# Order of scores, reciprocals and rotary sums within each part of the layer 2 self-attention of a four-layer decoder on one Trainium2 core

## The reference, cut to what matters

```
qkv = jnp.einsum('bsd,dhf->bshf', x, w_qkv) + b_qkv
q, k, v = jnp.split(qkv, 3, axis=-1)
q = q * cos + _rotate_half(q) * sin
k = k * cos + _rotate_half(k) * sin
...
scores = jnp.einsum('bhqd,bhkd->bhqk', q, k) / jnp.sqrt(jnp.float32(f))
...
scores = scores + alibi[None]
scores = jnp.where(causal == 0, -1000000000.0, scores)
weights = jax.nn.softmax(scores, axis=-1)
attn = jnp.einsum('bhqk,bhkd->bhqd', weights, v).transpose(0, 2, 1, 3)
return jnp.einsum('bshd,hdm->bsm', attn, w_out) + b_out
```

## Time and profile before

| what | value |
|---|---|
| median of 3 runs | 3147.62 us (3141.78 to 3148.28) |
| the profiled execution, its own time | 3148.16 us |
| its span in the profile | 3146.4 us |
| mean granted TensorE clock | 0.861 of full |
| stretch of this self-attention | some 1508 to 2030 us of the span |
| PE, DVE, ACT, POOL busy in that stretch | 424.41, 244.59, 312.20, 275.52 us of 522.00 |

### The profile page before, as it was taken

The page is one execution under the profiler, slowest core; times in us unless marked ns, Lnnn a source line. Parts: engine busy times, 40 slices in busy tenths (PEclk is TensorE's granted clock), DMA queues, the critical chain, the costliest instruction groups (busy, mean ns, idle before and its releaser), DMA issues. The chain is left out here.

```text
span 3146.4 us, 40958 instructions
## 1 busy us (share of the span) xinstructions
PE 2411.6 (77%) x12416; PEld 1417.6 (45%) x12416; DVE 1811.8 (58%) x4431; ACT 1239.4 (39%) x2575; POOL 534.3 (17%) x509
## 2 busy tenths in 40 slices
PE   6763976666768998699688888775888879578587
PEld 4653642224623323366344444453444456557454
DVE  4666347778855576444544444345666643745777
ACT  2442342224344454322466666523444422223212
POOL 0410000003310000000455555342000000043100
PEclk7875977777879999799799999877999989688799
DMA  0000000001010000000322222000000000100000
GB/s 32 31 6 0 1 5 0 0 0 44 1 55 1 0 0 0 0 0 0 97 69 68 68 68 68 22 31 24 1 0 0 0 1 0 56 23 1 1 1 14
DMA packets 19876, 61.81 MB, mean 20 GB/s; under 512 B 4928, under 2 KB 4928, under 8 KB 18592
## 3 DMA queue, kind: packets, MB, share of 16 engines
q1 hardware_dynamic: 19488, 59.53, 6.0%
q10 hardware_dynamic: 256, 0.68, 0.1%
HBM read 42.37 MB, written 1.05 MB: 14 GB/s over the span
## 5 line engine op out<-in xcount | busy, mean ns | idle before, releaser
L689 DVE TENSOR_REDUCE MF<-P 128x1 f32<-128x512 f32 (+3 forms) x512 | 282.3, 587 | 97.4 <-PE P L479 53.3
L824 ACT ACTIVATE PT<-P 128x512 f32<-128x512 f32 (+3 forms) x512 | 244.2, 516 | 232.5 <-PE P L496 123.0
L2318 PE MATMUL P<-XT,W 128*128 x424 | 221.0, 618 | 63.4 <-ACTq L2352 63.4
L2394 DVE SCALAR_TENSOR_TENSOR X<-P,WE,X 128x128 f32 x576 | 162.5, 344 | 167.0 <-PE P L2335 162.0
L2335 PEld LDWEIGHTS P<-W,e_h 128*128 128x128 f32 (+1 forms) x1952 | 220.7, 191 | 61.1 <-issue 53.2
L2335 PE MATMUL P<-W,e_h 128*128 128x128 f32 (+1 forms) x1952 | 227.8, 278 | 3.3 <-DVE X L2394 3.3
L1286 POOL TENSOR_TENSOR d_e<-d_e,d_rc 128x512 f32<-128x512 f32 (+3 forms) x256 | 178.2, 723 | 223.1 <-DVE d_rc L1193 223.0
L2363 ACT ACTIVATE e_g<-P 128x512 f32<-128x512 f32 x148 | 88.4, 597 | 310.5 <-PE P L2318 310.5
L496 PE MATMUL P<-QA,KA 128*128 128x512 bf16 (+3 forms) x512 | 180.2, 358 | 32.6 <-ACT PT L824 12.7
L479 PE MATMUL P<-KA,QA 128*128 128x512 bf16 (+3 forms) x512 | 182.2, 362 | 28.3 <-ACT KA L808 15.1
L541 PE MATMUL P<-PT,VA 128*32 128x512 f32 (+3 forms) x1024 | 195.8, 518 | 0.0
(11 more groups left out here) (359 smaller groups left out, 4635.5 us busy)
## 6 DMA issues: line engine op xcount, KB each, us to landing
d_bt<-in_alibi SPq DMA_DIRECT2D x32, 512.0 KB, 3.7
d_moved<-d_raw SPq DMA_DIRECT2D x256, 64.0 KB, 2.0
W<-in_w_L_xattn SPq DMA_DIRECT2D x1, 4291.0 KB, 14.1
W<-in_w_L_ffn SPq DMA_DIRECT2D x1, 3333.0 KB, 11.1
W<-in_w_L_ffn SPq DMA_DIRECT2D x1, 3155.0 KB, 10.2
W<-in_w_L_attn SPq DMA_DIRECT2D x1, 2636.0 KB, 11.6
W<-in_w_L_ffn SPq DMA_DIRECT2D x1, 2310.0 KB, 9.0
W<-in_w_L_ffn SPq DMA_DIRECT2D x1, 1744.0 KB, 6.9
```

The costliest lines, as they stand in the source:

```text
L689: last = v.tensor_reduce(col, src, AX.X, ALU.max, negate=True)
L824: a.activation(k.PT[0:self.kp, h % self.slots, t, N - w:N], src, ACT.Exp, scale=self.scale).then_inc(s("exp_done"), 1)
L2318: pe.matmul(P[:, PG + j % 2, :], w["w1"][:, col:col + 128], x, start=True, stop=True).then_inc(s("gate"), 1)
L2394: last = v.scalar_tensor_tensor(x, y, k.WE[:, bass.ds(c * 4 + t, 1), e], x, ALU.mult, ALU.add)
```

## The change

On PE, `scores` moves from before `values`, `result` and `weighted` to the end of each part. On DVE, both calls of `recip` move ahead of `biased`. On POOL, `rope` moves ahead of `shares`. ACT and SP stay as they are. No instruction is added or taken away, and every wait stays with its instruction.

```diff
@@ PE, line 1145
                     if 0 <= n - 3 < ITEMS:
                         turn(n - 3, j)
-                    if 0 <= n - 2 < ITEMS:
-                        scores(n - 2, j)
                     if j == 1 and 0 <= n - 2 < ITEMS:
                         values(n - 2)
                     if j == 1 and 0 <= n - 5 < ITEMS:
                         result(n - 5)
                     if 0 <= n - 4 < ITEMS:
                         weighted(n - 4, j)
+                    if 0 <= n - 2 < ITEMS:
+                        scores(n - 2, j)
@@ DVE, line 1205
-                    if 0 <= n - 2 < ITEMS:
-                        biased(n - 2, j)
                     if j >= 1 and 0 <= n - 2 < ITEMS:
                         recip(n - 2, j - 1)
                     if j == 0 and 0 <= n - 3 < ITEMS:
                         recip(n - 3, QT - 1)
+                    if 0 <= n - 2 < ITEMS:
+                        biased(n - 2, j)
@@ POOL, line 1288
+                    if j % 2 == 1 and 0 <= n - 1 < ITEMS:
+                        rope(n - 1, j // 2)
                     if j >= 1 and 0 <= n - 2 < ITEMS:
                         shares(n - 2, j - 1)
                     if j == 0 and 0 <= n - 3 < ITEMS:
                         shares(n - 3, QT - 1)
-                    if j % 2 == 1 and 0 <= n - 1 < ITEMS:
-                        rope(n - 1, j // 2)
```

## The result

| | before | after |
|---|---|---|
| median of 5 runs | 3147.62 us | 3171.21 us (3164.99 to 3177.44) |
| ratio to before | | 1.0081, 95% interval 1.0062 to 1.0100 |
| profiled execution, its own time | 3148.16 us | 3171.21 us |
| its span | 3146.4 us | 3169.4 us |
| mean granted TensorE clock | 0.861 | 0.856 |

The change makes the kernel slower: by 0.81% in the ratio, by 23.6 us between the two medians. The forecast was 3173 us.

A forecast was written before the change was run, and what follows sets the result against it. PE was taken to bound layer 2 self-attention, idling 2.62 us per 15.05 us item in a loop through ACT, DVE and POOL. Longer loop +15, low clock +22 - 9.5, stage ends -2: +25.5, so 3173 us; range 3154 to 3184.

The forecast's parts named there:

- The old loop is cut: POOL: sum of keys waits for one pair of shares, ends 6.3 to 6.8 us behind projection; 1.75 us wait goes.
- The new wait: PE ahead of the projection of keys: idles 2.6 us for ACT's copy of values, 3.43 us from scores of part 1.
- The wait ahead of the scores of part 3: PE: 0.6 us of idling stay there, 4.11 us from the projection of keys to these scores.
- The new loop: PE's item period: 4.11 + 8.01 + 3.43 = 15.55 us, 0.50 more than before; 30 rounds give +15 us.
- The clock: Low TensorE clock after the idle stretch in three of four items: 22 x 1.0 = +22 us, less 9.5 of before.
- The rival that went by every item: Low clock in all 30 items of the layer 2 self-attention: +36.5 us, 3184 us; chance 0.12.
- The sum: Whole kernel: 15 + 22 - 9.5 - 2 = +25.5 us, all in the layer 2 self-attention; 3173 us.
- the 2 us taken: Start and end of the stage: first keys come ahead of a pair of shares, -2 us, bounds 0 and -4.
- The rivals: Layer 2 self-attention: clock as before 0.14, every item 0.12, clock never falling 0.08, faster hand-over 0.07, old loop uncut 0.03.
- no hand-over was shorter: Rival at the projection of keys: scores to values copy under 2.9 us; with 2.5 us, -15 us, 3132 us; chance 0.07.

The follow-up runs named there:

- The swap on ACT: Changed kernel with ACT's copy of the values moved ahead of the exponentials of part 1; 3090.00 us, ratio 0.9813.
- the fastest kernel: Changed kernel with ACT's copy of the values ahead of the exponentials and PE's scores of part 1 right behind the values; 3069.69 us, ratio 0.9747.

## Why the prediction was right, and where its terms were off

**The old loop is cut.** Right. The wait of 1.75 us is gone; the sum of keys ends 6.25 us behind the projection, a little earlier than the 6.3 to 6.8 predicted, since the sum was taken at 1.77 us and takes 1.27: the contention with DVE's products was in the rows before, and the prediction didn't ask whether it would stay.

**The new wait.** Right in place, releaser and size: 2.55 us (predicted 2.6), 3.46 us from the scores of part 1 to the projection (1725.64 to 1729.10; predicted 3.43). The 3.40 us of the earlier trace rows, read where PE was idle, gave it. The swap on ACT, and the two edits that moved the scores of part 1 alone, show that this is the cause.

**The wait ahead of the scores of part 3.** 0.56 us (predicted 0.6); from the projection to these scores 4.08 us (predicted 4.11).

**The new loop.** Predicted 15.55 us, measured 15.35 where the clock stayed high. The term at fault is the stretch of PE's own work: 8.01 us were taken from the old order, 1717.83 to 1725.64 is 7.81. The spacing of two groups depends on their neighbours: the transposes of part 1 take 0.71 us up to the values (1722.25 to 1722.96) where they took 0.81 up to the scores, and the values 0.90 (1722.96 to 1723.86) where they took 1.00 behind the scores (1714.41 in the earlier trace rows, up to 1715.41). The two groups of PE before that follow those values, and end at the projection of keys (1717.19):

```profile
1715.41 1.06 PE L1138 MATMUL P<-W,d_ot 128*128 128x128 f32 x8
1716.39 0.87 PE L1127 MATMUL P<-d_pt,d_vp 128*64 128x384 f32 x4
```

So an item with a high clock takes +0.30 us and not +0.50: PE waits 0.49 us longer (3.11 less 2.62), and its own work fits into 0.2 us less, a term that the prediction took to be unchanged.

**The clock.** The sum of keys goes from 1572.41 to 1993.54 in 26 items, 421.1 us; at 15.35 they would take 399.1. So the low clock costs 22.0 us after, against 9.5 before. Twenty low stretches begin within these 26 items, so 1.10 us each (some reach into the next item). Predicted were three in four of 30 items, at 1.0: also 22. The share of three in four was a choice between the 6 of 26 before and all, which no row fixed, so that it came out is in part luck; and 20 at 1.10 come to the same as 22 at 1.0.

The Trainium skill, TensorE: Matmul & The Clock Gate, section "HAM oscillation — how this bites in real kernels", tells of a loop in which the clock fell in every turn. The prediction read from it that all 30 items would be slow. But the waits of that loop are longer than the 2.55 us here, so that page doesn't say it of this kernel. The trace agrees with it in kind, and not in number: 20 in 26 items, and every second item in the kernel with the new order on PE alone. The rival that went by every item had 3184 us.

**The sum.** Per steady item +0.30 at a high clock and +0.48 for the clock (22.0 less 9.5, over 26) make +0.78; 26 of them are 20.4 us. The start of the stage gained 0.5 us and its end 1.8, together near the 2 us taken. That is +18.1 in the stage, where +25.5 was predicted: 6 of the difference are the 0.20 us in each of 30 rounds, most of the rest the steady rounds being 26 and not 30. The profiled execution is longer by 23.0 us. The other 5 us lie outside the stage: it starts 2.6 us later, at its first GpSimd row 1515.56 instead of 1512.95, and 2.3 us come behind it. No instruction changed there, and the other traces show that this much comes by itself: in the twelve kernels, which are the same up to this stage, its first GpSimd row starts anywhere from 1508.83 to 1518.32 us, and what follows the stage's last DVE row (X<-X,P) up to the end of the span takes 1120.1 to 1123.3 us. So the total fitted within 2 us by luck: the stage itself was forecast 7 us too high, and 5 us of chance made up for most of it.

**The rivals.** None held. That of a clock that falls in every item was nearest, and no hand-over was shorter than the rows had shown.

## What to carry to other kernels

When instructions are moved on one engine, follow each wait of the instruction that now comes right behind them, and read on the waiting side's engine what stands in front of its releaser: the copy of the values needed nothing from the scores, but stood behind exponentials that did. A duration in the trace before that includes contention with another engine is not a constant either: look whether the new order still lets the two overlap, as with the sum of keys (1.77 and 1.27 us). The size of the new wait can be read from a place in the trace before where the engine had too little work to cover that chain. Split a change that touches several engines, since here two of its three parts were worth 1.7% and the third took back more than that.

## What the runs showed of the hardware that was not expected

- Useless matmuls can pay. One a round in idle time took 13 us off the kernel before (0.43%, interval 0.30 to 0.57), and two a round 29 us off the changed one, with the granted clock at 1.00 throughout the steady part.
- A low stretch of the clock can cost next to nothing: with waits behind it that take it up, and a sum of keys that takes 0.5 us less behind it (before, with part 1's scores late), items of 17.2 to 17.9 us with a low stretch stood beside 17.48 us with a high clock. The price of a low stretch was 1.58 us before, 1.64 in the changed kernel with the values copied first (15.17 or 15.18 less 13.54), 1.3 with PE's order alone (17.7 less 16.41), 1.10 in the changed kernel and some 0.1 here.
- The same idle stretch of 2.55 us was followed by a low clock in 20 of 26 items of the changed kernel, but in exactly every second one with PE's order alone. What decides between them I didn't find out.
- The same group of eight matmuls, the values, took 0.90 or 1.00 us from its start to the next, by its neighbours: 0.90 between transposes and results (changed kernel), 1.00 behind scores (before). What stands behind it counts as well. In the fastest kernel the values stand behind transposes, as in the changed one, but ahead of scores, and take 0.99, and the results behind these scores 1.09, where they took 0.98 behind values in both kernels (1715.41 to 1716.39 before, 1723.86 to 1724.84 after). PE of the fastest kernel:

```profile
1700.31 1.06 PE L1098 MATMUL P<-W,XT 128*128 128x128 f32 x8
1701.30 0.92 PE L1117 MATMUL P<-d_kr,d_qr 64*128 64x384 f32 x4
1702.14 1.16 PE L1138 MATMUL P<-W,d_ot 128*128 128x128 f32 x8
1703.23 0.87 PE L1127 MATMUL P<-d_pt,d_vp 128*64 128x384 f32 x4
```
